# Front of a chained transformer kernel: bias rows on 16 partitions, category loads ahead of layer rows, tokens as the stationary operand

## What is computed

```python
x = x + L0_attn(L0_cond(x, itok_B_0_8, ...), Wq, bq, Wk, bk, Wv, bv, Wo, bo)        # adapter by language id, then windowed attention
x = x + L0_ffn(L0_cond2(x, itok_B_2_61, weight, bias), W1, b1, A1, B1, R1, ...)     # per-category matrix, then LoRA mixture
x = x + L1_attn(L1_cond(x, itok_B_0_2, ...), Wq[0:8], bq, ..., bo, ..., b2, ...)    # experts, then eight attention layers
x = x + L1_ffn(L1_cond2(x, itok_B_0_2, ...), ...)                                   # experts, then three trees and attention

def L0_cond2(x, category_ids, weight, bias):     # weight (64, 128, 128)
    W = weight[category_ids]                     # one matrix for each of the 32 batches
    return einsum('bli,bio->blo', x, W) + bias[category_ids][:, None, :]
```

## Time and profile before

| | us |
|---|---|
| median of 3 runs | 699.86 |
| lowest and highest run | 694.5, 703.19 |
| profiled execution, first to last instruction (its span; the page gives no other time of it) | 701.3 |
| PE busy (matrix products) | 613.4 (87%) |
| DVE busy | 435.5 (62%) |
| ACT busy | 318.0 (45%) |
| POOL busy | 117.5 (17%) |

### The profile page before, as it was taken

How to read it: one execution, slowest core, us unless ns; L and a number is a source line. 1 busy time by engine, 2 the same in 40 slices (tenths; PEclk the granted TensorE clock), 3 DMA queues, 4 the chain that set the end, 5 groups by cost and what they waited for, 6 DMA issues and landing times.

```text
span 701.3 us, 9366 instructions
## 1 busy us (share of the span) xinstructions
PE 613.4 (87%) x3221; PEld 424.0 (60%) x3234; DVE 435.5 (62%) x1024; ACT 318.0 (45%) x504; POOL 117.5 (17%) x94
## 2 busy tenths in 40 slices
PE   9577899999999888989897979798849989999996
PEld 4355767877775555545463637354538868465595
DVE  4989333477776667666658484856664577644444
ACT  4064112343435556565656555656524424444441
POOL 0320131042300111111020111110150354200000
PEclk9789879899999999999999999999987997999997
DMA  3011396300005001010101010100000000000000
GB/s 91 22 46 46 83 264 157 69 0 1 0 1 150 1 1 46 1 46 1 45 0 45 0 45 0 45 0 0 1 1 1 1 0 1 0 1 0 1 0 31
DMA packets 43867, 21.83 MB, mean 31 GB/s; under 512 B 14642, under 2 KB 40941, under 8 KB 43834
## 3 DMA queue, kind: packets, MB, share of 16 engines
q1 hardware_dynamic: 43834, 21.40, 11.4%
HBM read 20.79 MB, written 0.52 MB: 30 GB/s over the span
## 4 chain that ended last, share of the span: by engine, by line
PE 43%; issue 29%; DVE 19%; POOL 5%; ACT 2%; POOLq 0%; DVEq 0%
PE ps L1508 8%; PE ps L1525 7%; POOL rstd L495 5%; PE ps L1712 5%; PE ps L1730 4%; PE ps L1736 2%; DVE z L1025 2%; DVE zr L1066 2%; PE ps L1386 2%; PE ps L1262 1%; DVE xn L850 1%; PE ps L1592 1%; PE ps L1399 1%; PE ps L1426 1%; DVE stat L830 1%
## 5 line engine op out<-in xcount | busy, mean ns | idle before, releaser
L495 POOL TENSOR_TENSOR rstd<-rv,minus_half 128x4 f32<-128x4 f32 x34 | 47.6, 1400 | 305.2 <-DVE rv L839 305.2
L1066 DVE SCALAR_TENSOR_TENSOR zr<-ps,zr 128x512 fp32r<-128x512 f32 x96 | 64.1, 689 | 52.9 <-ACT zr L666 52.4
L666 ACT ACTIVATE zr<-ps 128x512 fp32r<-128x512 f32 x96 | 57.5, 599 | 83.4 <-PE ps L1508 79.8
L1598 PEld LDWEIGHTS ps<-wl,z 128*128 128x128 f32 x512 | 64.0, 192 | 17.5 <-ACT z L728 8.7
L1592 PE MATMUL ps<-cf,wl 128*128 128x512 f32 x128 | 68.1, 636 | 6.9 <-ACT cf L574 6.9
L824 DVE TENSOR_TENSOR yt<-ps,z 128x512 f32<-128x512 f32 x32 | 22.1, 692 | 80.2 <-ACT z L733 42.4
L1598 PE MATMUL ps<-wl,z 128*128 128x128 f32 x512 | 68.4, 276 | 0.0
L1525 PE MATMUL ps<-zr 128*128 128x512 f32 x192 | 61.4, 401 | 6.3 <-DVE zr L1066 6.3
L1508 PE MATMUL ps<-zr 128*128 128x512 f32 x192 | 64.7, 420 | 1.0 <-DVE zr L1007 1.0
L1219 DVE SCALAR_TENSOR_TENSOR z<-z,kc 128x512 f32<-128x512 f32 x48 | 34.5, 751 | 44.5 <-ACT z L781 43.1
L574 ACT ACTIVATE cf<-ps,vl 128x512 f32<-128x512 f32 x32 | 24.9, 778 | 69.5 <-PE ps L1578 69.5
(11 more groups left out here) (251 smaller groups left out, 1098.7 us busy)
## 6 DMA issues: line engine op xcount, KB each, us to landing
wl<-in_L_attn_W SPq DMA_DIRECT2D x16, 256.0 KB
big<-in_L_cond_weight SPq DMA_DIRECT2D x32, 64.0 KB, 1.8
arena<-in_L_cond_expert_wi SPq DMA_DIRECT2D x1, 1024.0 KB, 5.7
arena<-in_L_cond_expert_wo SPq DMA_DIRECT2D x4, 256.0 KB, 7.0
big<-in_L_ffn_q_w SPq DMA_DIRECT2D x2, 512.0 KB, 6.6
big<-in_L_ffn_k_w SPq DMA_DIRECT2D x2, 512.0 KB, 7.9
tree_v<-in_L_ffn_v_w SPq DMA_DIRECT2D x2, 512.0 KB, 6.7
arena<-in_L_cond_share_wi SPq DMA_DIRECT2D x1, 768.0 KB, 7.0
```

What stands on the lines that cost most here:

```text
L495: nc.gpsimd.tensor_tensor(rstd[:, half, :], rv[:, half, :], minus_half[:, :], ALU.pow).then_inc(S_["rstd"], 1)
L666: nc.scalar.activation(hidden_part(h, n, 0), ps[h][:, n % 2, :], ACT.Relu).then_inc(S_[k + "_hi"], 1)
L1066: V.scalar_tensor_tensor(hidden_part(h, n, 1), ps[h][:, n % 2, :], 0.0, hidden_part(h, n, 0), ALU.max, ALU.subtract).then_inc(S_[k + "_lo" ...
L1598: ins = T.matmul(ps[h][:, 2, tok(h, i)], z(h, c)[:, tok(h, i)], wl[s][:, 4 * D + FF + c * D:4 * D + FF + (c + 1) * D], start=False, stop=( ...
```

## The change

- `row_bias` and its parts stand on 16 partitions of 128 elements (eight rows of `bo`, eight of `b2`) instead of on one partition of 2048. DVE's five operations stay where they are in the stream, and so does DVE's wait for `ld_rb`.
- In SP's stream the 32 category loads are written out instead of looped, and they, the mixture's weights and the experts' weights stand ahead of the 14 loads of `rows` and the three loads of `bias3`. The functions `load_mixture` and `load_ffns` hold the same loads as before.
- POOL adds `token_bias` before the roots and writes the sum to `xt[1]`, after a wait for DVE's last mask (`a_mask`).
- The category products take the 32 tokens of a batch as the stationary operand, at one of four column positions of the array, and move the 128x128 matrix through them. The result has tokens on the partitions, so ACT copies it to `xn` and PE turns it back, four transposes for each half, before DVE adds the bias.
- The turn of `rows` and its copy to `cols` move from the front into the second half of the mixture.

```diff
-        row_bias = Z[1][0:1, 4:8, :].rearrange("p a n -> p (a n)")
-        row_parts = Z[1][0:1, 8:14, :].bitcast(BF16).rearrange("p a n -> p (a n)")
+        row_bias = Z[1][0:2 * LAYERS, 4, 0:D]
+        row_parts = Z[1][0:2 * LAYERS, 8, :].bitcast(BF16)
...
+            def load_mixture():
+                load(gvec[:, 0, :], I["L1_cond_gate_vecs"], "ld_gv")
...
+                load(w2f[:, :, 0:D], I["L0_ffn_W2"].rearrange("(c p) n -> p c n", p=P), "ld_d")
...
             for n, name in enumerate(("bo", "b2")):
-                load(row_bias[:, n * LAYERS * D:(n + 1) * LAYERS * D],
-                     I["L1_attn_" + name].rearrange("(a l) d -> a (l d)", a=1), "ld_rb")
+                load(row_bias[n * LAYERS:(n + 1) * LAYERS, :], I["L1_attn_" + name], "ld_rb")
+            sp.wait_ge(S_["ld_ids"], 48)
+            for b in range(B):
+                cat = sp.value_load(ids[0:1, 1, b:b + 1], min_val=0, max_val=CATS - 1)
+                sp.dma_start(w_cat[:, b:b + 1, :],
+                             I["L0_cond2_weight"][bass.ds(cat, 1), :, :].rearrange("a p n -> p a n")
+                             ).then_inc(S_["ld_cat"], 16)
+            load_mixture()
+            load_ffns("L1_cond_expert_wi", "L1_cond_expert_wo", L1E, 0, "ld_e")
+            load_ffns("L1_cond_share_wi", "L1_cond_share_wo", L1S, L1E, "ld_e")
+            load(gate1[:, :, :], I["L1_cond_gate_w1"].rearrange("(c p) n -> p c n", p=P), "ld_e")
+            load(gate2[:, :], I["L1_cond_gate_w2"], "ld_e")
...
             sp.wait_ge(S_["p_rb"], 5)
             for part in range(3):
-                load(bias3[part:part + 1, :, :].rearrange("p l d -> p (l d)"), row_part(part), "ld_rb")
-
-            sp.wait_ge(S_["ld_ids"], 48)
-            with sp.Fori(0, B) as b:
-                cat = sp.value_load(ids[0:1, 1, bass.ds(b, 1)], min_val=0, max_val=CATS - 1)
-                sp.dma_start(w_cat[:, bass.ds(b, 1), :],
...
+                load(bias3[part:part + 1, :, :], row_part(part), "ld_rb")
...
+            pool.wait_ge(S_["ld_b"], 16 * 5)
+            pool.wait_ge(S_["a_mask"], 2 * LCH)
+            for h in HALVES:
+                nc.gpsimd.tensor_tensor(xt[1][:, h], xt[0][:, h], token_bias[:, :].unsqueeze(1).to_broadcast([P, TILES, D]),
+                                        ALU.add).then_inc(S_["p_pool"], 1)
             for h in HALVES:
                 root(h + 1, h)
-            pool.wait_ge(S_["ld_b"], 16 * 5)
-            for h in HALVES:
-                nc.gpsimd.tensor_tensor(xt[0][:, h], xt[0][:, h], token_bias[:, :].unsqueeze(1).to_broadcast([P, TILES, D]),
-                                        ALU.add).then_inc(S_["p_pool"], 1)
...
-            act.wait_ge(S_["p_mm"], PREP["cols"])
-            copy(cols[:, :], ps[1][:, 1, 0:P], "p_mmc")
...
-                copy(xf[:, h], ps[h][:, 3, :], "b_xf")
+                copy(xf[:, h], ps[h][:, 3, :], "c_act")
+            for h in HALVES:
+                act.wait_ge(S_["c_pe"], h + 1)
+                copy(xn[:, h].rearrange("p i d -> p (i d)"), ps[h][:, 0, :], "c_act")
...
                 mixture_out(1, h)
+            act.wait_ge(S_["p_mm"], PREP["cols"])
+            copy(cols[:, :], ps[1][:, 2, 0:P], "p_mmc")
...
-                residual(h, ps[h][:, 2, :], xt[0], xt[1], "b_res")
...
-                dve.wait_ge(S_["c_mm"], h + 1)
-                V.tensor_tensor(by_batch(cf[:, h]), by_batch(ps[h][:, 0, :]), spread(cbias_b[:, h * HB:(h + 1) * HB], S),
+                residual(h, ps[h][:, 2, :], xt[1], xt[1], "b_res")
...
+                dve.wait_ge(S_["c_pe"], 2 + h + 1)
+                V.tensor_tensor(by_batch(cf[:, h]), by_batch(ps[h][:, 2, :]), spread(cbias_b[:, h * HB:(h + 1) * HB], S),
...
-            pe.wait_ge(S_["ld_rows"], 16 * (LV + TREES))
-            turn(ps[1][:, 1, :], [rows[:, :]], "p_mm")
-
-            pe.wait_ge(S_["p_mmc"], PREP["cols"])
...
-                pe.wait_ge(S_["b_xf"], h + 1)
+                pe.wait_ge(S_["c_act"], h + 1)
                 for b in range(HB):
-                    ins = T.matmul(batch(ps[h][:, 0, :], b), w_cat[:, h * HB + b, :], batch(xf[:, h], b),
-                                   start=True, stop=True)
-                ins.then_inc(S_["c_mm"], 1)
+                    i, q = divmod(b, P // S)
+                    ins = T.matmul(ps[h][q * QUAD:(q + 1) * QUAD, 0, tok(h, i)], batch(xf[:, h], b), w_cat[:, h * HB + b, :],
+                                   start=True, stop=True, tile_position=(0, q * QUAD))
+                ins.then_inc(S_["c_pe"], 1)
+            for h in HALVES:
+                pe.wait_ge(S_["c_act"], 2 + h + 1)
+                turn(ps[h][:, 2, :], [xn[:, h, i, :] for i in range(TILES)], "c_pe")
...
             lora_out(0)
+            pe.wait_ge(S_["ld_rows"], 16 * (LV + TREES))
+            turn(ps[1][:, 2, :], [rows[:, :]], "p_mm")
             pe.wait_ge(S_["p_gw"], 3)
...
-            keep_warm(6, ps[1][:, 2, :])
+            keep_warm(6, ps[0][:, 3, :])
```

More of the change, by code:

```diff
@@ L276, in network @@
             x_tr x_f a_hid a_relu a_mask a_out a_tr a_cond var rstd xn
-            b_qk b_k b_rep b_qe b_vr b_vx b_sc b_sub b_exp b_pt b_ctx b_ctxc b_out b_res b_tr b_xf
-            c_mm c_out d_r1 d_z d_e d_zt d_ztc d_zl d_hid d_relu d_r2 d_out d_res d_tr d_xf
+            b_qk b_k b_rep b_qe b_vr b_vx b_sc b_sub b_exp b_pt b_ctx b_ctxc b_out b_res b_tr c_act
+            c_pe c_out d_r1 d_z d_e d_zt d_ztc d_zl d_hid d_relu d_r2 d_out d_res d_tr d_xf
             e_xl e_w e_hid e_hi e_lo e_acc e_accc e_accd e_gx e_p1 e_p1c e_p2 e_p2c e_sum e_g1 e_g1c e_g2 e_gw e_gl e_ge e_out
@@ L303, in row_part @@
         def row_part(n):
-            return row_parts[:, n * 2 * LAYERS * D:(n + 1) * 2 * LAYERS * D]
+            return row_parts[:, n * D:(n + 1) * D]
         def second_out(h):
@@ L356, in row, with load_ffns @@
                 return I[name].rearrange("(a n) -> a n", a=1)
+            def load_mixture():
+                load(gvec[:, 0, :], I["L1_cond_gate_vecs"], "ld_gv")
+                for e in range(ME):
+                    load(ar1[:, e * MR:(e + 1) * MR], I["L0_ffn_A1"][e], "ld_d")
+                    load(w2f[:, :, D + e * MR:D + (e + 1) * MR], I["L0_ffn_A2"][e].rearrange("(c p) r -> p c r", p=P), "ld_d")
+                load(ar1[:, MER:MER + ME], I["L0_ffn_R1"], "ld_d")
+                load(w2f[:, :, D + MER:D + MER + ME], I["L0_ffn_R2"].rearrange("(c p) e -> p c e", p=P), "ld_d")
+                sp.wait_ge(S_["k_mem"], 6)
+                for r in range(0, 3 * QUAD, QUAD):
+                    load(lora[r:r + MER, 0:FF], I["L0_ffn_B1"].rearrange("e r n -> (e r) n"), "ld_d")
+                    load(lora[r + MER:r + MER + 1, 0:FF], row("L0_ffn_b1"), "ld_d")
+                    load(lora[r:r + MER, FF:], I["L0_ffn_B2"].rearrange("e r n -> (e r) n"), "ld_d")
+                    load(lora[r + MER:r + MER + 1, FF:], row("L0_ffn_b2"), "ld_d")
+                load(w1f[:, :], I["L0_ffn_W1"], "ld_d")
+                load(w2f[:, :, 0:D], I["L0_ffn_W2"].rearrange("(c p) n -> p c n", p=P), "ld_d")
+            def load_ffns(wi, wo, n, at, sem):
+                load(arena[:, at:at + n, 0, :], I[wi][0:n].rearrange("e d f -> d e f"), sem)
+                for e in range(n):
+                    load(arena[:, at + e, 1, :].rearrange("p (c n) -> p c n", c=FC),
+                         I[wo][e].rearrange("(c p) n -> p c n", p=P), sem)
             load(kc[:, 0:K_GOAL], konst[:, 0:K_GOAL], "ld_const")
@@ L461, in _ @@
                 load(leaf_b2[t * QUAD:t * QUAD + LEAVES, :], I[f"L1_ffn_{q}_b2"], "ld_n")
-            sp.wait_ge(S_["c_mm"], 2)
+            sp.wait_ge(S_["c_pe"], 2)
             for t, q in enumerate("qkv"):
```

## The result

The changed kernel takes 732.31 us in the median of 4 runs (730.11 to 732.47), the kernel before 698.66 on the same chip (4 runs, 694.5 to 703.19): a ratio of 1.047, 95% interval 1.041 to 1.053. It is slower by 33.7 us.

A forecast was written before the change was run, and what follows sets the result against it. PE held 43% of the chain, DVE 19%, no transfer. Span 701.3 + 45.6 (wait) + 1 (attention) - 7.5 (products) + 0.4 (turn of `rows`) = 740.8; the profiled span is 1.4 above the median, so 739 us; range 728 to 750.

The forecast's parts named there:

- The wait that decides: DVE's wait for `ld_rb` ahead of `key_bias`: the late `bias3` loads make it run at 83.8 instead of 38.22, 45.6 us later.
- Rival B: SP's unrolled category loads cost only 0.40 us each, `key_bias` at 59.8, 715 us; chance 0.07 for anything under 728.
- The whole of it lands on the path: At `key_bias`: nothing of the next stages can go ahead, so the whole 45.6 us delay lengthens the path.
- The early edits count zero: Front, ahead of `key_bias`: bias split gains at most 6.8 to 7.8 us, only lengthening DVE's wait, so counted at zero.
- Attention after the wait: Attention, begun by PE at 1.2 GHz after its idle time: costs between nothing and 4 us, 1 taken.
- The category products: Category products through the mixture's start: products take 3.7 us instead of 11.74; gain 7.5 us, between 2 and 10.5.
- The copied row: Profile row of attention's context product, 32 passes of 32 columns at four positions in 0.46 us, scaled to the category products.
- The earlier category, mixture and expert weights do not help anybody: Weight loads moved ahead in SP's queue: no gain, since PE finds these weights ready before, too.
- Rival A: Whole kernel faster: the front's edits count and DVE's wait ahead of `key_bias` does not bind, 687 us; chance 0.02.
- rival C: Slower still: column positions not side by side at low clock, 752 us, or rows loads 13 longer; chance 0.11 above 750.

The follow-up runs named there:

- the first experiment: The changed kernel with the three `bias3` loads issued behind the eighth category load instead of behind all weights: 683.01 us, 0.978 of before.

## Why the prediction was right

Direction, mechanism and size held: 739 us forecast, 732 measured, inside the range. One term, the gain of the category products, came out beyond its bounds, the others were off by 2 us or less, and one sentence holds only because of the wait. Both larger errors point the same way, so the forecast isn't right because errors cancel.

- **The wait that decides**: right, 43.7 us instead of 45.6. Of its parts: the category loads 1.12 us each (1.15 taken); the mixture 56.97 - 47.75 = 9.2 (10.6), the experts 13.1 (12.5), the rows 8.7 (9.7), `bias3` 1.9, landing 1.74 (1.6). Rival B, 0.40 a load, is out: 1.12 was measured, and register load and address arithmetic stand one behind the other in SP's stream. With the loop 0.37 us a load went, more than its branch of 45 ns and its register operation of 64; the prediction's 1.38 left out the counting step (37 ns) and the gaps. The Trainium skill (Advanced Engine Details and Errata, Control Flow Timing) states about 108 ns for a compare-and-branch; that alone would, by estimate, have left 1.38 a load.
- **The whole of it lands on the path**: right. Moving the three loads, or dropping the wait, gives back all 49 us.
- **The early edits count zero**: right. Without its wait `key_bias` would have run at 81.88 - 49.05 = 32.83, 5.4 us earlier than before, under the bound of 6.8 to 7.8; the wait took all of it. The split of the rows took 3.3 us (14.57 to 17.84) instead of 0.5 to 1.5: two of its five operations, beside POOL's add (14.82 to 17.44), took 1.17 and 1.26 us where the same two forms took 0.21 and 0.28 just before. PE's half of the adapter came later still, so nothing hung on it.
- **Attention after the wait**: 0.44 us (1 taken), with the low clock where it was expected.
- **The category products**: right in kind, too small: 11.95 us (7.5 taken, 2 to 10.5 as bounds), and the products took 1.99 us where 3 to 5 was to be the sign. The copied row, 14.4 ns for 32 columns times four, gave 3.7 us; 128 columns cost 31 ns, not 58 (and the old products 11.74 us, not the 11.6 that the sum used). The factor of four of the Trainium skill (TensorEngine Tiling (Array Packing), Performance Considerations) gave 2.1 us by estimate, and the run shows about that; with four in a row at one position it was 4.31. And the clock stayed at 2.4 GHz, which is the 3.5 us that I had put down as an extra. This term (4.5 us) and the wait's (1.9) make up most of the 7.0 us by which the lag at the experts' first product, 32.5 us (155.88 at L1512 in the chain, where L1508 of before stands at 123.40), is under the 39.5 forecast.
- **"The earlier category, mixture and expert weights do not help anybody: PE finds them ready before, too"**: true of the changed kernel, but only because of the wait; wrong as a reason. There PE comes to the mixture at 126.14, long after even the old order has the weights in place (87.19 in the kernel with the products alone). Where nothing delays attention, products that end 10 us sooner do not find them ready, and alone gained nothing measurable: there the gain needs both edits, and I had credited the products with all of it. This didn't move the forecast, where the wait binds.

Rival A's time, 687, is what the edits give where the wait doesn't bind: 683, with the front as it put it and the products larger. Of rival C nothing came: the positions run side by side, the clock stayed up, and the 14 rows loads behind the experts' weights took 8.7 us, less than the 9.7 before.

The version with the three loads moved, at 683 us, is faster than the kernel before by about 15 us and than the changed kernel by 49; the runs with these loads at three places (issued from 20.9, 23.8 and, without the wait, 79.9 us) all took 682 to 683 us, so their place is free as long as nobody waits for them.

## What to carry to other kernels

A transfer that is small, and was early, becomes the bound when its queue is reordered: walk the new order instruction by instruction, sum the issue times up to it, and compare with who waits for it and when; here that one sum gave the sign, and a move of three loads turned +4.7% into -2.2%. When a step on the path is made faster, ask of the next step whether its inputs come that much earlier too, and add to the wait what a low clock behind it costs. What an engine finds ready before the change is no evidence for after.

## What was not expected of the hardware

DVE's small operations stood still beside POOL's. In the first experiment, POOL's timeline:

```profile
78.26 2.35 POOL L523 TENSOR_TENSOR arena_r<-arena,zr 128x1024 fp32r<-128x1024 f32 x1
...
81.67 2.35 POOL L523 TENSOR_TENSOR arena_r<-arena,zr 128x1024 fp32r<-128x1024 f32 x1
```

And DVE's, beside it:

```profile
78.73 1.90 DVE L965 SCALAR_TENSOR_TENSOR logit<-logit,small 128x12 f32<-128x12 f32 x1
...
82.02 2.03 DVE L965 SCALAR_TENSOR_TENSOR logit<-logit,small 128x12 f32<-128x12 f32 x1
```

DVE's ends, 80.63 and 84.05, are POOL's ends, 80.61 and 84.02, to 0.03 us; with POOL out of the way the same operation took 0.17. The Trainium skill (SBUF — State Buffer, Who interferes with whom) says that a DVE instruction with two inputs in SBUF contends with a GpSimd instruction that reads SBUF; these rows agree. In the changed kernel a DVE operation with one tensor and a scalar per partition as inputs (3x4, `gvec`) met the same: 2.24 us, ending at 129.10 where POOL's ends at 129.08, against 0.22 in the first experiment with POOL out of its way. Weights that arrive earlier let POOL start earlier, and so moved this contention onto DVE's gate steps, where in the kernel before POOL's split began at 100.58, after these steps; here it cost nothing measurable.

The idle time of PE nearly cost its length twice: in the kernel with the products alone, 4.9 us of waiting were followed by 4.1 us more in the next two steps, at 1.2 GHz instead of 2.4; with the weights earlier both were gone.
